# Causal scores of a chunked linear attention: one head per 32-row quarter of the TensorE array

## The chip, the core and the metric

The kernel runs on one core of a Trainium2 chip. The metric is the device time of one execution in microseconds. Engines are named as in the profile: PE is the TensorE matmul stream and PEld its weight loads, DVE is VectorE, ACT is ScalarE, POOL is GpSimd, SP is the engine that issues the DMAs.

## What is computed

One transformer layer over x of shape (2, 4096, 256) in float32: linear attention with 8 heads of 32 features in chunks of 64 tokens, then a mixture of 8 experts. The change touches only `scores`, which are masked causally inside a chunk.

```python
def step(state, inp):                      # b: 2 batches, h: 8 heads, c, e: 64 tokens of a chunk, d: 32 features
    qq, kk, vv = inp
    inter  = jnp.einsum('bhcd,bhde->bhce', qq, state)
    scores = jnp.einsum('bhcd,bhed->bhce', qq, kk) * mask     # mask = tril(ones(64, 64))
    intra  = jnp.einsum('bhce,bhed->bhcd', scores, vv)
    state  = state + jnp.einsum('bhcd,bhce->bhde', kk, vv)
    return (state, inter + intra)
...
x = x + _layernorm(attention(_layernorm(x)))
gate, up = x_n @ Wg[e], x_n @ Wu[e];  out = sum_e weights[e] * ((silu(gate) * up) @ Wd[e])
x = x + _layernorm(out)
```

## The kernel before

The 4096 rows of each batch are cut into 16 blocks of 256 rows, so a block holds 512 tokens, in four tiles of 128. A tile is half a block (`p` = 0 or 1) of one batch (`b`), and holds two chunks (`i` = 0 or 1). A software pipeline runs two blocks at once: while PE does the eight experts of block i-1, it does the attention of block i in between. The order is written out by hand: the list `STEPS` has 28 slots of attention steps, and `rest` (called in each engine's loop over the blocks) puts slots 4e-4+2m and 4e-3+2m between the products of expert e, half m. On PE one such turn is `up(e, m)` (gate and up products, 12 matmuls of 512 moving columns), a slot, `down(e-1, m)` (12 matmuls of 256 columns), a slot. Attention operands are plain fp32; the products with weights are float32r in three terms (high by high, low by high, high by low). A plain fp32 matmul that is no transpose leaves two weight loads and two matmuls in the trace: 64 matmuls are 128 records.

The steps around the change, in the order of the slots, and where they stand in the turns:
- `("kt", 0), ("kt", 1)` after `up(2, 1)`: PE transposes the keys (L530); ACT copies them out of PSUM to `kz` twice (L743), scaled by `odd_even[:, 0]` and by `odd_even[:, 1]`. These scales are 1 and 0 on alternating groups of 32 partitions, so copy `j` keeps only one head of each pair of heads and has zeros for the other.
- `("su", 0), ("su", 1)` after `up(3, 0)`: PE makes each chunk's key-value product (L573), DVE adds it to the running `state` (L951) and counts up `state_ready`.
- `("s", 0), ("s", 1)` after `up(3, 1)`: the scores. A matmul (L544) has 64 rows (two heads, one of them zeroed in `kz`), 64 stationary columns (the keys of a chunk) and 64 moving columns (its queries). Half `r` of the array's rows takes one pair of heads and writes bank `r` of two PSUM banks; chunk `i` takes half `i` of the output partitions. So four 64x64 tiles of the array are used in turn. A step has 2 (b) x 4 (n) x 2 (i) x 2 (r) = 32 matmuls. DVE multiplies each step's 128x1024 scores by the mask (L936) and counts up `prob_ready`.
- `("o", 0), ("o", 1)` after `up(4, 0)`: outputs, from the state and the queries (`with_state`, L446, 66 moving columns) and from the masked scores and the values (L461, 33 moving columns), also in 64x64 tiles.

PSUM: the attention has four banks, `att_ps`. Successive steps take banks 0 and 1, then 2 and 3, by turns (`att_half`), and each waits until the step before the last has been read out (`READ_OUT`). Block 0 has orders of its own (`FIRST_PE`, `FIRST_ACT`, `FIRST_DVE`), in which the two score steps stand apart from each other; `is_first(a)` tells it from the 15 other blocks.

Of the kernel before, what the change touches and what calls it, by code (L numbers as in the profile page):

```python
# [8 lines left out]

# [2 lines left out]

# [4 lines left out]
B, S, HID = 2, 4096, 256  # L19
H, D = 8, 32  # L20
E, INNER = 8, 256
P = 128
KT = HID // P
HG = H * D // P
# [92 lines left out]
def build_program(nc, x, wq_t, wkv_t, wo_t, norm_w, wg, wu, wd, wr, temperature, out):  # L117
# [4 lines left out]
    with ctx:  # L122
# [152 lines left out]
        def reach(eng, count, block, k):  # L275

            s, per_block, first = count
            base, offset = block
            value = offset * per_block + k + first
            if isinstance(base, int):  # L280
                if base * per_block + value > first:
                    eng.wait_ge(s, base * per_block + value)  # L282
            else:
                eng.wait_ge(s, base * per_block + value)
# [24 lines left out]
        def att_half(step, a):  # L309
# [3 lines left out]
                return att_ps[:, 2 * n, :]  # L313
            return att_ps[:, 2 * n:2 * n + 2, 0:256 if is_first(a) and step[0] == "q" else columns]

        def is_first(a):
            return psum_order(a) is FIRST_PSUM_STEPS


        def prob_of(p, a):  # L320
            return probs[1 - p if is_first(a) else p]


        def is_last(f):
# [107 lines left out]
        def _(pe):  # L432
# [19 lines left out]
            def o_own(p, dst, a):  # L452
                for b in range(B):
                    for x in range(2):
                        with_state(p, dst, b, x, x)
                for b in range(B):
                    for j in range(HPG):
                        for g in range(HG):
                            for i in range(2):
                                chunk, c = slice(C * i, C * i + C), b * HPG * VA + j * VA  # L460
                                last = nc.tensor.matmul(dst[C * g:C * g + C, i, c:c + VA],  # L461
                                                        prob_of(p, a)[chunk, j // 2, b, 2 * g + j % 2, :],
                                                        v_sb[chunk, 2 * p + b, g * HPG + j, :], start=False, stop=False)
                return last

# [14 lines left out]
            def att_step(step, a):  # L480
# [1 line left out]
                    return  # L482
                kind, dst, number = step[0], att_half(step, a), number_of(step, a)

                if number >= 2:
                    count, k = READ_OUT[psum_order(a)[number - 2]]
                    reach(pe, count, a, k)
                else:
                    count, k = READ_OUT[PSUM_STEPS[N_PSUM - 2 + (number + N_PSUM) % 2]]
                    reach(pe, count, (a[0], a[1] - 1), k)  # L490
# [41 lines left out]
                elif kind == "s":  # L532
                    p = step[1]
                    reach(pe, q_ready, a, p + 1 if is_first(a) else HG)
                    reach(pe, kz_ready, a, p + 1)
                    pe.sem_inc(quarters_begun, 1)
                    for b in range(B):
                        for n in range(2 * HG):
                            g, j = divmod(n, 2)
                            for i in range(2):  # L540
# [5 lines left out]
                                                            start=True, stop=True)  # L546
                elif kind == "o":
                    p = step[1]
                    reach(pe, prob_ready, a, p + 1)
                    reach(pe, v_ready, a, p + 1)  # L550
                    reach(pe, state_ready, a, p + 1)
                    pe.sem_inc(quarters_begun, 1)
# [154 lines left out]
        def _(act):  # L707
# [18 lines left out]
            def att_step(step, a):  # L726
# [9 lines left out]
                elif kind == "kv":  # L736
# [2 lines left out]
                    copy(v_sb[:, ts, :, 0:D], src[:, :, HID:2 * HID].rearrange("p b (h d) -> p b h d", h=H))\  # L739
                        .then_inc(v_ready[0], 1)  # L740
                elif kind == "kt":
                    for j in range(2):
                        last = nc.scalar.activation(kz[:, step[1], :, j, :], src, ACT.Copy, scale=odd_even[:, j:j + 1])  # L743
                    last.then_inc(kz_ready[0], 1)
# [150 lines left out]
        def _(dve):  # L895
# [5 lines left out]
            def low(dst, src, high_part):  # L901
                return nc.vector.tensor_tensor(dst, src, high_part.bitcast(f32), ALU.subtract)  # L902
# [22 lines left out]
            def att_step(step, a):  # L925
                kind = step[0]
                if kind == "xt":
# [2 lines left out]
                    lo, hi = (xt[:, :, half] if is_first(a) else halves(xt[:, k, :]) for xt in (xt_lo, xt_hi))  # L930
                    reach(dve, xt_hi_ready, a, k + 1)
                    low(lo, att_half(step, a), hi).then_inc(xt_ready[0], 1)
                elif kind == "s":
                    reach(dve, att_done, a, number_of(step, a) + 1)
                    each = [P, 2, 4 * HG, C]
# [416 lines left out]
```

## Time and profile before

| | |
|---|---|
| median of 3 runs | 1487.56 us (1487.32 to 1488.09) |
| the profiled execution | 1487.54 us |
| its span, first to last instruction | 1485.8 us |
| PE busy | 1462.7 us, 98% of the span, 14438 matmul records |
| DVE, ACT, POOL busy | 1003.5, 632.5, 427.4 us |
| granted TensorE clock, mean | 0.997 |

The profiled execution and the median are 0.02 us apart, so a sum made on the one holds for the other. The busy time of an engine is a union: records that overlap count once. A PE row of the timeline gives the start of its first record, the time to the modelled end of its last one, and the number of records; the distance between the starts of two neighbouring rows is how long the first of them held up the stream.

### The profile page before, as it was taken

What the parts mean: (1) busy time and instruction counts of PE and PEld (TensorE: products, weight loads), DVE (VectorE), ACT (ScalarE), POOL (GpSimd) and SP (SyncE); (2) the same over time, 40 slices, a digit from 0 to 9 for tenths busy, and PEclk for the clock granted to TensorE, in tenths of its full rate; (3) what the DMA queues carried; (4) which work ended last, traced back from release to release, by engine and by line L of the source; (5) the groups of instructions that cost most, each with busy time, mean ns of one, the idle gap of its engine ahead of it and who ended that gap; (6) DMA issues with size and microseconds to landing.
All of it is one profiled execution on the core that took longest, in us unless ns stands there. A gap on an engine that the chain in (4) does not pass through costs nothing. (4 is left out here: it accounts for less than half of the span.)

```text
span 1485.8 us, 37233 instructions
## 1 busy us (share of the span) xinstructions
PE 1462.7 (98%) x14438; PEld 1276.4 (86%) x14438; DVE 1003.5 (68%) x2397; ACT 632.5 (43%) x1157; POOL 427.4 (29%) x621
## 2 busy tenths in 40 slices
PE   7899999999999999999999999999999999999997
PEld 7788888888888888888888888888888888888886
DVE  6748567576676767667586675766667676675765
ACT  5434534444344443534435343443434445344332
POOL 1402414123241322414133141232413124141230
PEclk9999999999999999999999999999999999999999
DMA  5100000000000000000000000000000000000000
GB/s 172 58 2 15 14 0 14 14 14 14 0 28 0 14 14 14 14 0 14 14 14 14 0 14 14 14 14 0 28 0 14 14 14 14 0 15 16 2 8 22
DMA packets 25345, 24.59 MB, mean 17 GB/s; under 512 B 2016, under 2 KB 25056, under 8 KB 25312
## 3 DMA queue, kind: packets, MB, share of 16 engines
q1 hardware_dynamic: 25312, 24.13, 5.1%
q8 instruction: 23, 0.38, 0.1%
q14 instruction: 10, 0.08, 0.0%
HBM read 15.74 MB, written 8.39 MB: 16 GB/s over the span
## 5 line engine op out<-in xcount | busy, mean ns | idle before, releaser
L1013 DVE TENSOR_TENSOR late<-late,up_ps 128x512 f32<-128x512 f32 x256 | 174.9, 683 | 153.7 <-PE up_ps L440 149.3
L790 ACT ACTIVATE late<-gate_ps 128x512 f32<-128x512 f32 x256 | 152.6, 596 | 278.8 <-PE gate_ps L440 277.7
L440 PE MATMUL down_ps<-w_hi,h_hi 128*128 128x256 f32 x976 | 264.6, 293 | 0.0
L709 ACT ACTIVATE h_hi<-late 128x512 fp32r<-128x512 f32 x256 | 161.4, 630 | 222.0 <-DVE late L1013 221.9
L440 PE MATMUL down_ps<-w_hi,h_lo 128*128 128x256 f32 x976 | 253.9, 282 | 0.0
L1247 POOL TENSOR_TENSOR rms_in<-rms_in,minus_half 128x16 f32<-128x16 f32 x32 | 93.4, 2918 | 493.7 <-DVE rms_in L961 493.7
L902 DVE TENSOR_TENSOR h_lo<-late,h_hi 128x512 fp32r<-128x512 f32 x256 | 175.7, 686 | 65.4 <-ACT h_hi L709 65.4
L1035 DVE SCALAR_TENSOR_TENSOR late<-down_ps,route,late 128x256 f32<-128x256 f32 x364 | 158.6, 477 | 90.3 <-PE down_ps L440 87.8
L440 PE MATMUL gate_ps<-ft_hi,w_hi 128*128 128x512 f32 x512 | 204.0, 398 | 1.4 <-ACT ft_hi L709 0.8
L440 PE MATMUL gate_ps<-ft_hi,w_lo 128*128 128x512 f32 x512 | 203.0, 396 | 0.0
L440 PE MATMUL up_ps<-ft_hi,w_hi 128*128 128x512 f32 x512 | 199.7, 390 | 0.0
L440 PE MATMUL up_ps<-ft_hi,w_lo 128*128 128x512 f32 x512 | 199.5, 390 | 0.0
L440 PE MATMUL down_ps<-w_lo,h_hi 128*128 128x256 f32 x976 | 196.5, 283 | 0.0
L440 PEld LDWEIGHTS down_ps<-w_hi,h_hi 128*128 128x128 f32 x976 | 184.8, 189 | 10.5 <-issue 3.0
L440 PEld LDWEIGHTS down_ps<-w_hi,h_lo 128*128 128x128 f32 x976 | 185.8, 190 | 4.4
L440 PE MATMUL gate_ps<-ft_lo,w_hi 128*128 128x512 f32 x512 | 159.0, 392 | 0.0
L440 PE MATMUL up_ps<-ft_lo,w_hi 128*128 128x512 f32 x512 | 157.7, 389 | 0.0
L440 PEld LDWEIGHTS down_ps<-w_lo,h_hi 128*128 128x128 f32 x976 | 151.5, 191 | 0.0
L440 PEld LDWEIGHTS gate_ps<-ft_lo,w_hi 128*128 128x128 f32 x512 | 96.5, 188 | 21.9
L440 PEld LDWEIGHTS up_ps<-ft_hi,w_hi 128*128 128x128 f32 x512 | 96.4, 188 | 21.1
L440 PEld LDWEIGHTS up_ps<-ft_hi,w_lo 128*128 128x128 f32 x512 | 96.4, 188 | 20.1
L440 PEld LDWEIGHTS up_ps<-ft_lo,w_hi 128*128 128x128 f32 x512 | 96.2, 188 | 20.0
(172 smaller groups left out, 2420.6 us busy)
## 6 DMA issues: line engine op xcount, KB each, us to landing
xs<-in_x SPq DMA_DIRECT2D x32, 256.0 KB, 2.9
out_rows<-late SPq DMA_DIRECT2D x32, 256.0 KB, 2.2
late<-in_wg SPq DMA_DIRECT2D x7, 256.0 KB, 3.3
late<-in_wu SPq DMA_DIRECT2D x7, 256.0 KB, 4.3
late<-in_wd SPq DMA_DIRECT2D x6, 256.0 KB, 4.4
late<-in_wkv_t SPq DMA_DIRECT2D x1, 512.0 KB, 4.1
x<-in_wd SPq DMA_DIRECT2D x2, 256.0 KB, 5.2
late<-in_wq_t SPq DMA_DIRECT2D x1, 256.0 KB, 4.6
```

The costliest lines, as they stand in the source:

```text
L440: last = nc.tensor.matmul(dst, lhs, rhs, start=n == 0, stop=n == len(terms + low_terms) - 1)
L709: return nc.scalar.activation(dst, src, ACT.Copy)
L790: nc.scalar.activation(h_f[:, m, :], gate_ps[:, :], ACT.Silu).then_inc(silu_ready[0], 1)
L902: return nc.vector.tensor_tensor(dst, src, high_part.bitcast(f32), ALU.subtract)
L1013: nc.vector.tensor_tensor(h_f[:, m, :], h_f[:, m, :], up_ps[m][:, :], ALU.mult).then_inc(h_ready[0], 1)
L1035: last = nc.vector.scalar_tensor_tensor(dst[:, t, :], src, route[:, t, e:e + 1], acc[:, t, :], ALU.mult, ALU.add)
L1247: nc.gpsimd.tensor_tensor(rms_f[:, p, :, :], rms_in[:, p, :, :], minus_half[:, :, :], ALU.pow)\
```

## The change

For all blocks but the first, a score matmul takes one head alone, on 32 rows: head `j` of a group of four lies on the 32 partitions of row quarter `j`, and its scores go to PSUM bank `j`. Chunk `i` still takes output half `i`, so eight 32x64 tiles of the array are used in turn: four quarters for chunk 0, four for chunk 1. Both halves `p` lie side by side in the four banks, columns 0 to 255 and 256 to 511, so the two steps together fill `att_ps`. The number of matmuls stays: 2 (b) x 2 (g) x 2 (i) x 4 (j) = 32 a step. Since no head has to be zeroed, ACT copies the transposed keys to `kz` once, unscaled. The waits follow the banks: both score steps wait until all four banks are free (`state_ready` 2), DVE masks neither half before both steps are done on PE, and the output steps wait until both halves are masked. The masked scores get another layout in SBUF, `prob_block`. The first block stays as it was.

```diff
--- before.py
+++ after.py
@@ -9,6 +9,7 @@
 
 
 
+import itertools
 import math
 from contextlib import ExitStack
 
@@ -313,12 +314,23 @@
                 return att_ps[:, 2 * n, :]
             return att_ps[:, 2 * n:2 * n + 2, 0:256 if is_first(a) and step[0] == "q" else columns]
 
+
+        def score_banks(p):
+            return att_ps[:, :, 256 * p:256 * p + 256]
+
         def is_first(a):
             return psum_order(a) is FIRST_PSUM_STEPS
 
 
         def prob_of(p, a):
             return probs[1 - p if is_first(a) else p]
+
+
+        def prob_block(p, a, chunk, b, g, j):
+            if is_first(a):
+                return prob_of(p, a)[chunk, j // 2, b, 2 * g + j % 2, :]
+            return prob_of(p, a).rearrange("p r b n c -> p (r b n c)").rearrange("p (j b g c) -> p j b g c", j=HPG, b=B,
+                                                                                 g=HG)[chunk, j, b, g, :]
 
 
         def is_last(f):
@@ -459,7 +471,7 @@
                             for i in range(2):
                                 chunk, c = slice(C * i, C * i + C), b * HPG * VA + j * VA
                                 last = nc.tensor.matmul(dst[C * g:C * g + C, i, c:c + VA],
-                                                        prob_of(p, a)[chunk, j // 2, b, 2 * g + j % 2, :],
+                                                        prob_block(p, a, chunk, b, g, j),
                                                         v_sb[chunk, 2 * p + b, g * HPG + j, :], start=False, stop=False)
                 return last
 
@@ -482,7 +494,10 @@
                     return
                 kind, dst, number = step[0], att_half(step, a), number_of(step, a)
 
-                if number >= 2:
+                if kind in ("s", "o") and not is_first(a):
+
+                    pass
+                elif number >= 2:
                     count, k = READ_OUT[psum_order(a)[number - 2]]
                     reach(pe, count, a, k)
                 else:
@@ -533,8 +548,16 @@
                     p = step[1]
                     reach(pe, q_ready, a, p + 1 if is_first(a) else HG)
                     reach(pe, kz_ready, a, p + 1)
+                    if not is_first(a):
+
+                        reach(pe, state_ready, a, 2)
                     pe.sem_inc(quarters_begun, 1)
-                    for b in range(B):
+                    for b, g, i, j in itertools.product(range(0 if is_first(a) else B), range(HG), range(2), range(HPG)):
+                        head, c = slice(D * j, D * j + D), b * P + C * i
+                        tok, out_c = 2 * p * P + c, (b * HG + g) * C
+                        last = nc.tensor.matmul(score_banks(p)[C * i:C * i + C, j, out_c:out_c + C], kz[head, p, g, 0, c:c + C],
+                                                q_t[head, g, tok:tok + C], start=True, stop=True)
+                    for b in range(B if is_first(a) else 0):
                         for n in range(2 * HG):
                             g, j = divmod(n, 2)
                             for i in range(2):
@@ -546,7 +569,7 @@
                                                             start=True, stop=True)
                 elif kind == "o":
                     p = step[1]
-                    reach(pe, prob_ready, a, p + 1)
+                    reach(pe, prob_ready, a, p + 1 if is_first(a) else 2)
                     reach(pe, v_ready, a, p + 1)
                     reach(pe, state_ready, a, p + 1)
                     pe.sem_inc(quarters_begun, 1)
@@ -739,6 +762,9 @@
                     copy(v_sb[:, ts, :, 0:D], src[:, :, HID:2 * HID].rearrange("p b (h d) -> p b h d", h=H))\
                         .then_inc(v_ready[0], 1)
                 elif kind == "kt":
+                    if not is_first(a):
+                        copy(kz[:, step[1], :, 0, :], src).then_inc(kz_ready[0], 1)
+                        return
                     for j in range(2):
                         last = nc.scalar.activation(kz[:, step[1], :, j, :], src, ACT.Copy, scale=odd_even[:, j:j + 1])
                     last.then_inc(kz_ready[0], 1)
@@ -930,6 +956,15 @@
                     lo, hi = (xt[:, :, half] if is_first(a) else halves(xt[:, k, :]) for xt in (xt_lo, xt_hi))
                     reach(dve, xt_hi_ready, a, k + 1)
                     low(lo, att_half(step, a), hi).then_inc(xt_ready[0], 1)
+                elif kind == "s" and not is_first(a):
+
+                    reach(dve, att_done, a, number_of(("s", 1), a) + 1)
+                    each = [P, HPG, B * HG, C]
+                    nc.vector.tensor_tensor(prob_of(step[1], a).rearrange("p r b n c -> p (r b n c)")
+                                            .rearrange("p (j n c) -> p j n c", j=HPG, c=C),
+                                            score_banks(step[1]).rearrange("p j (n c) -> p j n c", c=C),
+                                            causal[:, :, :].unsqueeze(1).broadcast_to(each), ALU.mult)\
+                        .then_inc(prob_ready[0], 1)
                 elif kind == "s":
                     reach(dve, att_done, a, number_of(step, a) + 1)
                     each = [P, 2, 4 * HG, C]
```

The rows that follow are the built programs' order, each engine for itself, with the semaphores that an instruction waits for. On PE, around the two score steps, `att_ps<-q_t,kz`, between `up(3, 1)` and `down(2, 1)`. Before:

```order
L440 MATMUL up_ps<-ft_lo,w_hi 128x512 [waits ft_ready]
L440 MATMUL up_ps<-ft_lo,w_hi 128x512
L544 MATMUL att_ps<-q_t,kz 64x64 [waits kz_ready,state_ready,q_ready]
L544 MATMUL att_ps<-q_t,kz 64x64 x31
L544 MATMUL att_ps<-q_t,kz 64x64 [waits kz_ready,state_ready,q_ready]
L544 MATMUL att_ps<-q_t,kz 64x64 x31
L284 REGISTER_ALU [waits h_lo_ready]
L440 MATMUL down_ps<-w_hi,h_hi 128x256 [waits down_read]
```

And with the change:

```order
L452 MATMUL up_ps<-ft_lo,w_hi 128x512 [waits ft_ready]
L452 MATMUL up_ps<-ft_lo,w_hi 128x512
L558 MATMUL att_ps<-q_t,kz 64x64 [waits state_ready,q_ready,kz_ready]
L558 MATMUL att_ps<-q_t,kz 64x64 x31
L558 MATMUL att_ps<-q_t,kz 64x64 [waits state_ready,q_ready,kz_ready]
L558 MATMUL att_ps<-q_t,kz 64x64 x31
L285 REGISTER_ALU [waits h_lo_ready]
L452 MATMUL down_ps<-w_hi,h_hi 128x256 [waits down_read]
```

The 64 matmuls keep their place and number, and the names waited for are the same. What differs is the count: `("s", 0)` now waits for the second of the two state steps.

On ACT, at the copies of the transposed keys, `kz<-att_ps`, between the SiLU of expert 2's second half and the copy `h_hi` behind it. Before:

```order
L790 ACTIVATE late<-gate_ps 128x512 [waits h_lo_ready]
L284 REGISTER_ALU
L743 ACTIVATE kz<-att_ps,odd_even 128x2x256 [waits att_done]
L743 ACTIVATE kz<-att_ps,odd_even 128x2x256
L284 REGISTER_ALU
L743 ACTIVATE kz<-att_ps,odd_even 128x2x256 [waits att_done]
L743 ACTIVATE kz<-att_ps,odd_even 128x2x256
L709 ACTIVATE h_hi<-late 128x512 [waits down_done,h_ready]
```

With the change:

```order
L816 ACTIVATE late<-gate_ps 128x512 [waits h_lo_ready]
L285 REGISTER_ALU
L732 ACTIVATE kz<-att_ps 128x2x256 [waits att_done]
L285 REGISTER_ALU
L732 ACTIVATE kz<-att_ps 128x2x256 [waits att_done]
L732 ACTIVATE h_hi<-late 128x512 [waits down_done,h_ready]
```

Two of the four copies are gone; `h_hi` moves up by two instructions.

On DVE, at the masks, between expert 3's product `late<-late,up_ps` and the low half `h_lo`. Before:

```order
L1013 TENSOR_TENSOR late<-late,up_ps 128x512 [waits up_done,silu_ready]
L284 REGISTER_ALU
L936 TENSOR_TENSOR rows<-att_ps,causal 128x1024 [waits att_done]
L284 REGISTER_ALU
L936 TENSOR_TENSOR shared<-att_ps,causal 128x1024 [waits att_done]
L1035 SCALAR_TENSOR_TENSOR late<-down_ps,route,late 128x256 [waits down_done]
L1035 SCALAR_TENSOR_TENSOR late<-down_ps,route,late 128x256
L902 TENSOR_TENSOR h_lo<-late,h_hi 128x512 [waits h_hi_ready]
```

With the change:

```order
L1048 TENSOR_TENSOR late<-late,up_ps 128x512 [waits up_done,silu_ready]
L285 REGISTER_ALU
L963 TENSOR_TENSOR rows<-att_ps,causal 128x1024 [waits att_done]
L963 TENSOR_TENSOR shared<-att_ps,causal 128x1024 [waits att_done]
L1070 SCALAR_TENSOR_TENSOR late<-down_ps,route,late 128x256 [waits down_done]
L1070 SCALAR_TENSOR_TENSOR late<-down_ps,route,late 128x256
L928 TENSOR_TENSOR h_lo<-late,h_hi 128x512 [waits h_hi_ready]
```

The masks keep their place and their size, 128x1024. The register instruction between them, which made the count that the second mask waits for, is gone: both wait for the same count.

## Rows read from the trace of the kernel before

**Rows 1.** The page, its span, its engines and the granted clock in 40 slices.

```profile
span 1485.8 us, 37233 instructions
...
PE 1462.7 (98%) x14438; PEld 1276.4 (86%) x14438; DVE 1003.5 (68%) x2397; ACT 632.5 (43%) x1157; POOL 427.4 (29%) x621
...
PEclk9999999999999999999999999999999999999999
```

**Rows 2.** Busy time of each engine in one block's stretch, start of scores to start.

```profile
core 0: us, PE busy (x) PEld busy (x) DVE busy (x) ACT busy (x) POOL busy (x), PEclk, DMA share, GB/s
640.14:730.05 89.91, 89.91 (x895) 78.43 (x894) 61.37 (x147) 38.59 (x71) 26.67 (x38) 1.00 0.04 12
```

**Rows 3.** Records of the tile kz: count, duration in ns, first and last start.

```profile
L544 PEld LDWEIGHTS att_ps<-q_t,kz x2048: 129/135/135, 24.1 to 1361.7; 64*64 64x64 f32 x187
L544 PE MATMUL att_ps<-q_t,kz x2048: 218/218/267, 24.1 to 1361.8; 64*64 64x64 f32 x187
L743 ACT ACTIVATE kz<-att_ps,odd_even x64: 679/690/717, 22.6 to 1351.6; 128x512 f32<-128x512 f32 x64
```

**Rows 4.** Timeline of PE in one later block: start, us, what, records.

```profile
725.00 1.16 PE L573 MATMUL att_ps<-v_sb,k_sb 64*64 64x66 f32 x64
...
729.91 0.61 PE L440 MATMUL up_ps<-ft_lo,w_hi 128*128 128x512 f32 x2
730.46 2.12 PE L544 MATMUL att_ps<-q_t,kz 64*64 64x64 f32 x128
732.51 0.38 PE L440 MATMUL down_ps<-w_hi,h_hi 128*128 128x256 f32 x1
...
736.87 0.46 PE L446 MATMUL att_ps<-state,q_t 64*64 64x66 f32 x16
737.16 1.08 PE L461 MATMUL att_ps<-v_sb,rows 64*64 64x33 f32 x64
738.06 0.44 PE L446 MATMUL att_ps<-state,q_t 64*64 64x66 f32 x16
738.32 1.09 PE L461 MATMUL att_ps<-v_sb,shared 64*64 64x33 f32 x64
739.23 0.82 PE L446 MATMUL att_ps<-state,q_t 64*64 64x66 f32 x32
739.98 0.39 PE L440 MATMUL down_ps<-w_hi,h_hi 128*128 128x256 f32 x1
```

**Rows 5.** Timeline of PE, first block (score step, state step) and warming matmuls.

```profile
24.13 1.16 PE L544 MATMUL att_ps<-q_t,kz 64*64 64x64 f32 x64 [0.69 <-ACT kz L743]
...
26.85 0.70 PE L573 MATMUL att_ps<-v_sb,k_sb 64*64 64x66 f32 x32
...
47.65 4.52 PE L478 MATMUL gate_ps<-ident 128*128 128x128 f32 x39
```

**Rows 6.** Timeline of PE, router products of the same block, 128x32 tiles.

```profile
778.61 0.40 PE L601 MATMUL att_ps<-ft_lo,wr_pad 128*32 128x128 f32 x8
778.83 0.40 PE L601 MATMUL att_ps<-ft_hi,wr_pad 128*32 128x128 f32 x8
779.04 0.40 PE L601 MATMUL att_ps<-ft_lo,wr_pad 128*32 128x128 f32 x8
```

**Rows 7.** Weight loads of kz alone in two short stretches at the scores' start.

```profile
core 0: us, PEld busy (x), PEclk, DMA share, GB/s
730.46:730.48 0.03, 0.02 (x4) 1.00 0.00 0
730.48:730.51 0.03, 0.03 (x4) 1.00 0.00 0
```

**Rows 8.** Timeline of DVE from the state adds to the product behind the masks.

```profile
723.46 0.69 DVE L902 TENSOR_TENSOR h_lo<-late,h_hi 128x512 fp32r<-128x512 f32 x1 [0.22 <-ACT h_hi L709]
...
726.54 2.03 DVE L951 SCALAR_TENSOR_TENSOR state<-att_ps,odd_even,state 128x132 f32<-128x132 f32 x6
...
731.69 1.22 DVE L936 TENSOR_TENSOR rows<-att_ps,causal 128x1024 f32<-128x1024 f32 x1 [0.36 <-PE att_ps L544]
732.83 1.22 DVE L936 TENSOR_TENSOR shared<-att_ps,causal 128x1024 f32<-128x1024 f32 x1
734.24 0.88 DVE L1035 SCALAR_TENSOR_TENSOR late<-down_ps,route,late 128x256 f32<-128x256 f32 x2 [0.19 <-PE down_ps L440]
735.03 0.68 DVE L902 TENSOR_TENSOR h_lo<-late,h_hi 128x512 fp32r<-128x512 f32 x1
737.05 0.69 DVE L1013 TENSOR_TENSOR late<-late,up_ps 128x512 f32<-128x512 f32 x1 [1.34 <-PE up_ps L440]
```

**Rows 9.** Timeline of ACT at the copies of the transposed keys.

```profile
720.49 2.42 ACT L743 ACTIVATE kz<-att_ps,odd_even 128x512 f32<-128x512 f32 x4 [1.12 <-PE att_ps L530]
```

## The prediction, made blind

> **What bounds the kernel now.** Read first the page's engines [rows 1]: PE is busy for 1462.7 of 1485.8 us, and the clock reads 9 in all 40 slices, so the clock is not the subject. Then take one block by itself [rows 2]: from one start of the scores to the next are 89.91 us, and PE is busy in all of them, DVE in 61.4, ACT in 38.6. Fifteen of the sixteen blocks go like that. So PE's stream is the bound without a gap, and a microsecond taken out of it is a microsecond of the kernel, as long as no wait opens; a microsecond taken off ACT or DVE is worth nothing by itself.
>
> Next, how long the scores hold the stream [rows 4]: they start at 730.46, and `down` starts behind them at 732.51, so 2.05 us for 128 records; over the whole kernel these groups are 2048 records, 15 blocks of 128 and the first block's twice 64 [rows 3]. Fifteen times that is 31 us, about 2% of the kernel, and all that the change can take from is in it.
>
> **What sets the pace of the scores.** This decides the sum, so I take it from several rows.
>
> One score step alone, 64 records, has a row of 1.16 us [rows 5]; two steps, 128 records, have 2.12 [rows 4]. So 64 more records cost 0.96 us, 15.0 ns each, and 0.20 us is paid once. State products with 66 moving columns: 32 records 0.70 us [rows 5], 64 records 1.16 [rows 4], 14.4 ns each. Output products with 33 moving columns: 737.16 to 738.06 for 64 records [rows 4], 14.1 ns each. Half as many moving columns, and the same pace: so the columns that stream are not what binds.
>
> Now the whole array: 39 records of 128 stationary and 128 moving columns in 4.52 us [rows 5]. Less one duration (0.27) that is 4.25 / 38 = 112 ns each. A 64x64 tile has half the stationary columns, so on its own it should take about 56 ns; four tiles at once give 14.0. That is what the 64x64 rows show. In the router products the tiles are 32 columns wide and 128 columns move: 0.43 us for 16 records [rows 6], 27 ns each, again 112 / 4 = 28. So I read: each tile takes about 56 to 60 ns per record (here its weight load), and as many tiles work at once as there are tiles in turn, four in every row so far. The weight loads look like that too [rows 7]: four start within the first 25 ns of the scores, and none more in the next 30.
>
> **The change, part by part.**
>
> *The score matmuls.* Their number stays at 64 a block, 128 records, and so do 64 stationary and 64 moving columns; a record still costs its tile 56 to 60 ns. But there are now eight 32x64 tiles in turn. If all eight work at once, a record costs 14.0 / 2 to 15.0 / 2, I take 14.5 / 2 = 7.25 ns. Per block 128 x 7.25 = 0.93 us less. No row shows eight tiles at once, or 32-row quarters, so this price is bounded from both sides. Below: four loads start within 25 ns, some 6 to 8 ns from start to start [rows 7]; at 6.7 ns a record the gain would be 128 x 7.8 = 1.0 us. Above: if only two of the tiles in a column half worked at once and the other column half waited, 29 ns, a loss of 128 x 14.5 = 1.86 us. I take 7.25, because the price of one tile and the count of tiles have explained three shapes of tile (128x128, 128x32, 64x64), and the spacing of starts leaves room for eight in 56 ns. The amounts read at once do not grow either: two column halves times 128 partitions, before and after.
>
> Here the Trainium skill speaks against the change. Its page "TensorE: Matmul & The Clock Gate" (section "Wait — 56ns, not 53.3ns?") says that the distance between the starts of two matmuls never drops below about 25 ns, however small they are. By that rule 128 records would take 3.2 us, and no tiling could help. The trace does not agree: 14.1 to 15.0 ns in three groups of rows. The same page's section "Measured speedup vs the span model" has 4 row tiles at 3.07 times one, and 16 tiles at 10.6 times; no row here shows more than four.
>
> *Entering and leaving.* The 0.20 us paid once (filling, and the change to smaller tiles and back) I leave as it is: the tiles were small before.
>
> *The copies of the transposed keys.* Four copies in 2.42 us become two [rows 9], 1.2 us less on ACT a block, 18 us in all. Worth nothing: they end at 722.9, and the scores start at 730.46. What is next in that queue is `h_hi`, about a microsecond earlier; DVE waits 0.22 us for it [rows 8], and PE for neither.
>
> *The first score step waits for both state steps.* DVE ends its state adds at 728.57 [rows 8], PE comes to the scores at 730.46 [rows 4], with 1.9 us between. Nothing ahead of that point moves. Cost nothing; were the adds 1.9 us later, PE and all expert products behind it would stand.
>
> *Both masks wait for both steps.* DVE begins the first mask at 731.69 and ends the second at 734.05. The scores would end at 730.46 + 0.20 + 0.96 = 731.6, where they now end at 732.6: so the first mask starts where it does now although it waits for twice the work. Queued behind the masks are `add_down`, then the low half `h_lo`. `add_down` now waits 0.19 us for PE [rows 8]; `down` will be done earlier, so both start some 0.2 us sooner. A mask reads 256 columns of four banks in place of 512 of two; same 1024 elements, and I keep 1.22 us, with a tenth more or less as its bounds, which changes nothing.
>
> *The output steps wait for both masks.* PE comes to them at 736.87 now, at 735.94 then; the masks end at 734.05. The slack goes from 2.8 to 1.9 us. Were a mask 1 us longer, PE would wait here.
>
> *Other chains.* Only work that begins before the scores and is wanted after them loses 0.93 us of slack; the rest moves along with PE. The low half of expert 3 ends at about 735.5 and is wanted by `down(3, 0)` behind the outputs, at 739.98 less 0.93 [rows 4]. In a steady block PE shows no idle at all.
>
> *The first block* keeps its code.
>
> **Sum.** 15 blocks x 0.93 = 13.9 us from the profiled execution's 1487.54: 1473.6 us. The median of the runs is 1487.56, so the same number holds for it.
>
> **The rivals.**
>
> *Eight tiles, but a floor under them.* The starts within 25 ns come after a stretch in which instructions could queue up; over 256 instructions in a row PE may not be handed a load and a matmul every 7 ns. For it: the lowest pace held over a whole row is 14.1 ns. Against it: the pace did follow the tile's own time in every shape, with starts in a quick bunch and then a pause. A floor halfway, 10.9 ns, saves 128 x 3.6 = 0.46 us a block, 6.9 in all: 1480.6. Between 8 and 13 ns it gives 1475 to 1484.6.
>
> *The change doesn't do what it says: four at a time remain.* The number in flight may be a property of the engine, not of the tiles; four is all that any row shows. A record stays at 14.5 ns, the masks start 1 us later (their end at 735.0 against outputs at 736.87 hides it): 1487.5. The skill's 25 ns rule would end here too, since a floor that four tiles already reach leaves nothing to gain.
>
> *Slower: two at a time.* The order now puts four row quarters of one column half behind each other, then four of the other half. If quarters of one column half can share it only by twos, and PE does not look past them to the other half, a record costs 29 ns and a block 1.86 us more: 1487.5 + 27.8 = 1515.4. It decides from 14.5 ns a record on. Against it: `with_state` puts two tiles of one row half in a row, L461 two of one column half, and both hold the same pace: L446's 32 records hold the stream for 0.75 us with the change of shape in it [rows 4].
>
> **How the numbers follow.** Forecast 0.62, floor 0.18, four at a time 0.12, two at a time 0.08. The predicted time is the forecast's, 1473.6. Its own bounds are 6.7 ns (1472.5) and 8 ns (1475). The range goes from 1472 through the floor's cases to 1484.5 and holds 0.80; it leaves out no change and slower. A measurement of this kernel tells 0.2%, 3 us, from no change; so faster 0.80, same 0.12, slower 0.08.
>
> **What would show it.** In the changed profile: the row of the 128 score records at 1.1 to 1.2 us in place of 2.12, and `down` 1.1 us behind its start; a block at 89.0 us, with PE busy throughout; PE busy 14 us less in all; ACT 18 us less. A row of 1.6 us shows the floor, 2.1 four at a time, 4 two at a time. The masks should start 1.2 us after the scores' start as now; if PE idles ahead of L446's rows or ahead of the scores, one of the two added waits binds, and then my slacks of 1.9 us were wrong. The prediction fails most likely by the one price that no row shows, that of a record with eight tiles in turn.

## The result, and the profile after

The changed kernel takes 1482.63 us (median of 7 runs, 1481.39 to 1485.68), the kernel before 1487.95 (7 runs, 1487.32 to 1489.1). The ratio is 0.9968, 95% interval 0.9956 to 0.9979: faster by 5.3 us, which the interval holds clear of no change. The forecast was 13.9 us. The time lies inside the stated range of 1472 to 1484.5 us, but only because the range was drawn wide enough for the floor rival. The profiled execution took 1481.39 us, 6.15 less than the one before.

The page and one block's stretch of the changed kernel, to be held against [rows 1] and [rows 2]:

```profile
span 1479.7 us, 37189 instructions
...
PE 1456.3 (98%) x14438; PEld 1269.9 (86%) x14438; DVE 1000.7 (68%) x2397; ACT 612.6 (41%) x1127; POOL 431.6 (29%) x621
...
PEclk9999999999999999999999999999999999999999
```

```profile
core 0: us, PE busy (x) PEld busy (x) DVE busy (x) ACT busy (x) POOL busy (x), PEclk, DMA share, GB/s
637.37:726.89 89.52, 89.52 (x895) 78.05 (x893) 61.16 (x147) 37.28 (x69) 26.99 (x38) 1.00 0.04 12
```

A block, from one start of the scores to the next, went from 89.91 to 89.52 us, and PE is still busy in all of it. Fifteen times 0.40 is 6.0 us: the whole of the gain lies inside the blocks, and no new wait took part of it. It was not given back; it was smaller to begin with. PE's timeline around the scores shows where (start, us, what, records; [rows 4] before):

```profile
727.20 1.70 PE L558 MATMUL att_ps<-q_t,kz 32*64 32x64 f32 x128
728.84 0.39 PE L452 MATMUL down_ps<-w_hi,h_hi 128*128 128x256 f32 x1
...
733.21 0.46 PE L458 MATMUL att_ps<-state,q_t 64*64 64x66 f32 x16
```

The score row is 1.70 us, where 2.12 stood and 1.16 was forecast. DVE and ACT around it ([rows 8], [rows 9] before):

```profile
723.28 2.03 DVE L986 SCALAR_TENSOR_TENSOR state<-att_ps,odd_even,state 128x132 f32<-128x132 f32 x6 [0.15 <-DVEq L925]
...
728.94 1.23 DVE L963 TENSOR_TENSOR rows<-att_ps,causal 128x1024 f32<-128x1024 f32 x1 [0.87 <-PE att_ps L558]
730.08 1.22 DVE L963 TENSOR_TENSOR shared<-att_ps,causal 128x1024 f32<-128x1024 f32 x1
731.21 0.87 DVE L1070 SCALAR_TENSOR_TENSOR late<-down_ps,route,late 128x256 f32<-128x256 f32 x2
```

```profile
717.23 1.09 ACT L732 ACTIVATE kz<-att_ps 128x512 f32<-128x512 f32 x2 [1.12 <-PE att_ps L545]
```

How the pace runs inside the scores can be read by asking the timeline of the weight loads (PEld) for stretches that begin just ahead of the first load and end ever later: the count at the end of the row is how many loads have started by then. Here the stretches end 0.25, 0.50 and 0.75 us behind the first load. Before:

```profile
730.46 0.38 PEld L544 LDWEIGHTS att_ps<-q_t,kz 64*64 64x64 f32 x20 [0.35 <-issue]
...
730.46 0.62 PEld L544 LDWEIGHTS att_ps<-q_t,kz 64*64 64x64 f32 x36 [0.35 <-issue]
...
730.46 0.85 PEld L544 LDWEIGHTS att_ps<-q_t,kz 64*64 64x64 f32 x52 [0.35 <-issue]
```

With the change:

```profile
727.20 0.36 PEld L558 LDWEIGHTS att_ps<-q_t,kz 32*64 32x64 f32 x33 [0.35 <-issue]
...
727.20 0.62 PEld L558 LDWEIGHTS att_ps<-q_t,kz 32*64 32x64 f32 x49 [0.35 <-issue]
...
727.20 0.78 PEld L558 LDWEIGHTS att_ps<-q_t,kz 32*64 32x64 f32 x64 [0.35 <-issue]
```

Before, 20, 36, 52: an even 16 loads in each further quarter of a microsecond. With the change 33, 49, 64: the first quarter holds 33 loads, as eight tiles at once would have it, and then the pace is 15 to 16 per quarter, no better than before. Single starts in the trace say the same. The first 33 matmul records of a step start within 0.29 us; behind them the loads pause for about 0.13 us, then come stretches at 8.4 ns a record and stretches at 17; and the 65th record, the first of the second step, comes 106 ns behind the 64th.

### The profile page after: what moved, and what is told of

Same layout as the page of the kernel before. It is cut to its first block and busy times, and to the rows that moved or that the text cites. A ratio compares the mean times of both kernels' runs of the same rounds, so it can differ in the third digit from the quotient of the medians.

```text
span 1479.7 us, 37189 instructions
## 1 busy us (share of the span) xinstructions
PE 1456.3 (98%) x14438; PEld 1269.9 (86%) x14438; DVE 1000.7 (68%) x2397; ACT 612.6 (41%) x1127; POOL 431.6 (29%) x621
```

## The experiments

Theories. **F**, feeding: eight tiles do work at once, but PE is handed loads and matmuls slower than these tiles take them; about 32 records stand ready when the scores begin, the rest comes as it is handed on. **A**: batch 1's addresses are slow. **D**: row quarters of one column half share it by twos. **N**: neighbouring matmuls in one column half hinder each other. **Q**: the loss belongs to row quarters or to four banks at once. **T**: tiles are slowed by leftover work of earlier tiles. **J**: the waits between the two score steps cost. And the added waits and the copies, which were priced at nothing.

Each time below is a single execution, except that of `a_join`; the changed kernel's own seven executions differ by 4.3 us. The rows and the length of a block tell more: in the steady blocks of a trace they repeat to a few hundredths of a microsecond.

**Order of the same matmuls.** In `a_gb` the loops run g, b, i, j in place of b, g, i, j, in `a_ij` g, b, j, i (the ranges are shortened here to what they are in the 15 later blocks).

```diff
-for b, g, i, j in itertools.product(range(B), range(HG), range(2), range(HPG)):
+for g, b, i, j in itertools.product(range(HG), range(B), range(2), range(HPG)):      # a_gb
+for g, b, j, i in itertools.product(range(HG), range(B), range(HPG), range(2)):      # a_ij
```

> The changed kernel with the loop over the head groups g outside and that over the batches b inside: the same 64 score matmuls a block in another order. Theory F (a stock of 32 records, then handed on slowly): nothing changes, 32 records fast and 32 slow, row 1.70 us, time within 1 us of the changed kernel's 1481.4. Rival A (batch 1's addresses are slow): runs of 16 fast and 16 slow records alternate; sum and time the same, but the pattern inside the step is another.

> The changed kernel with the chunks i inside and the heads j outside of them, so that neighbouring matmuls take the two column halves of one row quarter, then the next quarter: same 64 matmuls a block, same eight tiles in turn. Theory F (feeding): no difference, row 1.70 us, period 89.51 us, time within 1 us of the changed kernel's. Rival N (neighbours in one column half hinder each other, as in the slower case of the prediction): the row gets shorter, by the 0.1 us of each stall or more.

Measured: 1482.26 and 1481.72 us. Timelines of PE, of `a_gb` and then of `a_ij`:

```profile
728.03 1.71 PE L558 MATMUL att_ps<-q_t,kz 32*64 32x64 f32 x128
```

```profile
727.28 1.71 PE L558 MATMUL att_ps<-q_t,kz 32*64 32x64 f32 x128
```

Not only the rows are the same. The starts of every eighth record lie within 3 ns of the changed kernel's (0, 106, 165, 223, 291, 458, 537, 604 ns in the first step), with the slow part behind the 32nd record each time, whichever batch and column half it belongs to. A and N fall.

**Four quarters of one column half.** `a_onehalf` leaves out chunk i = 1.

> The changed kernel without the scores of the second chunk of each 128 tokens (i = 1 is left out in the 15 later blocks, so half of the score work is missing): four 32x64 tiles in turn, all in one column half, 64 records a block. Forecast of the tile price: four row quarters of one column half work at once, one tile takes 58 ns a record, so 14.6 ns a record, score row about 1.15 us, 0.55 us less a block than the changed kernel, 1473 us. Rival D (quarters of one column half share it by twos): 29 ns a record, row about 2.0 us, 1486 us. Theory F has no say at 14.6 ns, since that is slower than it hands on.

Measured: 1475.13 us. PE's row, and the load counts at 0.25 and 0.50 us:

```profile
725.37 1.16 PE L558 MATMUL att_ps<-q_t,kz 32*64 32x64 f32 x64
```

```profile
725.36 0.38 PEld L558 LDWEIGHTS att_ps<-q_t,kz 32*64 32x64 f32 x20 [0.35 <-issue]
...
725.36 0.61 PEld L558 LDWEIGHTS att_ps<-q_t,kz 32*64 32x64 f32 x36 [0.35 <-issue]
```

1.16 us for 64 records, to the hundredth what 64 records of four 64x64 tiles take [rows 5], and the same counts of 20 and 36. So a tile of a row quarter costs what a 64x64 tile does, 58 ns a record, and four quarters in one column half do work at once. D falls, and the tile price of the prediction stands.

**Eight tiles without quarters.** `b_eight` is the kernel before with 64x32 tiles, eight in turn (the edit in short).

```diff
-for n in range(2 * HG):              # dst[C*i : C*i+64, r, ...],  kz[half, ..., c : c+64]
+for n in range(HG):
     ...
+    for h in range(2):               # dst[C*i+32*h : ... +32, r, ...],  kz[half, ..., c+32*h : ... +32]
```

> The kernel before with eight tiles of 64 rows and 32 columns in turn in place of four of 64x64: a score matmul of the 15 later blocks takes 32 keys and 64 queries of a head pair, and half of the scores is left out so that it stays at 128 records a block. No row quarters, two banks. It tells whether the eight tiles or the row quarters make the slow part. Theory F (feeding): eight tiles in turn take a record every 7.3 ns, the stock of 32 is gone, then stalls and 8.4 to 12 ns as in the changed kernel: row 1.70 us, block period about 89.5 us, time about 1481.5. Rival Q (the stall behind the 32nd record, 128 ns longer than in the run with small matmuls in four tiles, belongs to row quarters): no such stall, row 1.4 to 1.5 us, period 89.25 us, time about 1478.

Measured: 1480.32 us. PE's row, and the load counts at 0.25, 0.50 and 0.75 us:

```profile
727.12 1.62 PE L557 MATMUL att_ps<-q_t,kz 64*32 64x64 f32 x128
```

```profile
727.12 0.30 PEld L557 LDWEIGHTS att_ps<-q_t,kz 64*32 64x32 f32 x33 [0.35 <-issue]
...
727.12 0.60 PEld L557 LDWEIGHTS att_ps<-q_t,kz 64*32 64x32 f32 x54 [0.35 <-issue]
...
727.12 0.85 PEld L557 LDWEIGHTS att_ps<-q_t,kz 64*32 64x32 f32 x65 [0.35 <-issue]
```

33, then 54, then 65: the fast start and the fall of pace behind it come without a row quarter and with two banks instead of four. The stall that Q gave to the row quarters is there too: behind the 33rd load two gaps of 77 and 56 ns, where the changed kernel has 70 and 59. The row of 1.62 us is 0.08 short of the changed kernel's and 0.12 above what Q named, so Q falls as the main cause; 0.08 us a block may still belong to the shape.

**Short work for each tile.** `b_small` (four tiles of the kernel before) and `a_small` (eight row-quarter tiles) take 32 keys and 32 queries in each matmul.

> The kernel before (head pairs on 64 rows, four tiles in turn) with only the first 32 keys and 32 queries of each chunk in the score matmuls of the 15 later blocks, so three quarters of the scores are missing: 128 records a block as ever, but 32 stationary and 32 moving columns each, so a tile is free again after about half the time. It makes short work for a tile without any row quarter. Theory F (feeding): the same loss of pace as in the changed kernel appears without row quarters: 32 records fast, then 8 to 9 ns each with stalls, row about 1.7 us in place of 2.12, time about 1481.5. Rival Q (the loss belongs to row quarters or to four banks at once): the pace follows the tile, about 7 to 8 ns a record throughout, row about 1.2 us, time about 1474.

> The changed kernel with only the first 32 keys and 32 queries of each chunk in the score matmuls of the 15 later blocks (three quarters of the scores missing): row quarters, eight tiles in turn, each free again after half the time. Theory F: the tiles no longer matter, the first 32 records come as close as starts can, 6 to 7 ns, and behind them the pace is what PE is handed: the row stays between 1.6 and 1.75 us, time about 1481.5. If instead the slow part belongs to the time of the tiles, it halves: row about 1.2 us, time about 1474.5.

Measured: 1478.05 and 1478.15 us. PE's row of each, `b_small` first, with the load counts of `a_small` at 0.13, 0.25, 0.50 and 0.75 us behind:

```profile
726.16 1.47 PE L545 MATMUL att_ps<-q_t,kz 64*32 64x32 f32 x128
```

```profile
725.77 1.47 PE L558 MATMUL att_ps<-q_t,kz 32*32 32x32 f32 x128
```

```profile
725.77 0.23 PEld L558 LDWEIGHTS att_ps<-q_t,kz 32*32 32x32 f32 x30 [0.35 <-issue]
...
725.77 0.34 PEld L558 LDWEIGHTS att_ps<-q_t,kz 32*32 32x32 f32 x34 [0.35 <-issue]
...
725.77 0.59 PEld L558 LDWEIGHTS att_ps<-q_t,kz 32*32 32x32 f32 x60 [0.35 <-issue]
...
725.77 0.84 PEld L558 LDWEIGHTS att_ps<-q_t,kz 32*32 32x32 f32 x68 [0.35 <-issue]
```

Both expectations missed the size, and the pair says more than each. Both kernels need 1.47 us, though one has twice the tiles of the other, each half as long busy as in the changed kernel. In `a_small` the first 30 loads start within 0.13 us of the first one, 4 ns apart, and then PE has to wait: 34 after 0.25 us. So there is a floor that no tile sets, (1.47 - 0.19) / 128 = 10 ns a record over two steps (0.19 is the duration of one record here), and a stock of about 32 records ahead of it. In both kernels 0.16 to 0.17 us of it lie between the two steps, and the 64 records of one step start within 0.56 us, 8.9 ns apart.

The place of the stall says the same. The 33rd load of the first step starts 134 ns after the first in `a_small`, 195 in `b_eight`, 227 in the changed kernel and 245 in `b_small`, each as its tiles allow; the 34th starts after 244, 272, 297 and 277 ns. The first 33 differ by 111 ns, the next one by 53: it comes when it is handed on, nearly whatever the tiles do.

The changed kernel's 1.70 us lies 0.23 above that floor. Each of its steps takes about 0.13 us longer to start its 64 records, and its gap between the steps is 0.05 to 0.06 shorter. Its tiles' own 7.3 ns and the supply's pauses may add up in part instead of hiding each other; no run isolates that.

**Twice the matmuls.** `a_twice` and `b_twice` issue each step's score matmuls twice over, on the changed kernel and on the one before.

> The changed kernel with the score matmuls of each step issued twice over (same operands, same outputs) in the 15 later blocks: 256 records a block in place of 128, nothing left out. The question is where the changed kernel loses pace inside a step. Its trace shows a step's first 32 records at 7.3 ns each and the other 32 at over 12. Theory F (feeding): a stock of instructions stands ready when a step begins and is used up after 32 records; from then on PE is handed a record every 8 to 9 ns. Then the second pass has no fast part, 64 more records cost some 0.54 us a step, the score row goes from 1.70 to about 2.8 us, the time from 1481.4 to about 1498. Rival A (addresses): what is slow is the second half of a step, batch 1, by where its operands or outputs lie. Then fast and slow alternate a second time: 0.70 us more a step, the row about 3.1 us, the time about 1502.

> The kernel before with the score matmuls of each step issued twice over in the 15 later blocks: 256 records a block, four 64x64 tiles in turn, nothing left out. Beside the changed kernel doubled, which took 4.5 to 5.0 us for its 256 records with a pause of some 2 us ahead of about the 160th. Theory F with a supply that a pace of 14.6 ns a record doesn't exhaust: no pause, 128 more records cost 1.87 us, the row goes from 2.12 to about 3.99 us, the time from 1487 to about 1515. If the supply of instructions falls behind even that pace over a long stretch, pauses of 1 to 2 us show here too, and the row is 5 us or more, the time about 1530.

Measured: 1541.43 and 1536.95 us, 60 and 49 us above the kernels that they double. For `a_twice` 17 to 21 were expected; for `b_twice` 28, or 43 if pauses of 1 to 2 us showed, and they do. PE's timeline in one block of `a_twice`, and what the whole kernel's waits say:

```profile
195.57 1.97 PE L558 MATMUL att_ps<-q_t,kz 32*64 32x64 f32 x159
199.05 1.26 PE L558 MATMUL att_ps<-q_t,kz 32*64 32x64 f32 x97 [1.52 <-issue]
```

```profile
PE att_ps L558 <- issue: 24.5, 15, 2.1
```

The same of `b_twice`:

```profile
194.42 2.58 PE L544 MATMUL att_ps<-q_t,kz 64*64 64x64 f32 x159
197.91 1.67 PE L544 MATMUL att_ps<-q_t,kz 64*64 64x64 f32 x97 [0.91 <-issue]
199.50 0.39 PE L440 MATMUL down_ps<-w_hi,h_hi 128*128 128x256 f32 x1
```

```profile
PE att_ps L544 <- issue: 15.8, 14, 1.6
```

In 14 of the 15 later blocks of both, PE stops behind the 159th record, idle with nothing that the profile shows to wait for ("issue"), and goes on 3.37 to 4.06 us after the scores began in `a_twice` and 3.49 to 4.15 us in `b_twice`, although one came to that place in 1.97 us and the other in 2.58. Again the tiles do not set it. The trace shows what does. The profile counts the packets of a DMA queue of instructions; first the changed kernel's line, then that of `a_twice`, and `b_twice` has the same one:

```profile
q8 instruction: 23, 0.38, 0.1%
```

```profile
q8 instruction: 143, 2.34, 0.6%
```

The only code that grew is PE's, by 256 loads and matmuls a block, and this queue alone grew with it, so it carries PE's instructions; the other instruction queue stays at 10 packets. A steady block of the changed kernel has 1786 loads and matmuls in its trace, and no packet of instructions moves in that kernel between 151 and 1330 us: its blocks run from what was loaded before. With 2042 loads and matmuls, 9 packets of 16384 bytes move in a steady block. One of them falls into the scores. In the block of `a_twice` shown above it moves from 196.67 to 197.80 us, and PE (first column behind the length) goes on 1.25 us after it landed. The last columns are the DMAs' share and GB/s; 14 GB/s over 1.21 us is that packet:

```profile
core 0: us, PE busy (x) PEld busy (x) DVE busy (x) ACT busy (x) POOL busy (x), PEclk, DMA share, GB/s
195.57:196.60 1.03, 1.03 (x99) 1.03 (x101) 0.69 (x1) 0.13 (x1) 0.00 (x0) 1.00 0.00 0
196.60:197.81 1.21, 0.94 (x87) 0.80 (x71) 0.00 (x0) 0.50 (x1) 0.00 (x0) 1.00 0.06 14
197.81:199.05 1.24, 0.00 (x0) 0.00 (x0) 0.00 (x0) 0.00 (x0) 0.00 (x0) 1.00 0.00 0
```

Over all 29 pauses of the two runs PE goes on 1.24 to 1.61 us after such a packet has landed. In the last block the packets fall elsewhere, and so does the pause: in `a_twice` it stands behind the 130th record, and `b_twice` has none there and a row of 3.98 us, which is the 3.99 that F named. No run moved a packet on purpose, but these two blocks did it by themselves. So this second, longer pause is the loading of PE's instructions, and it is not part of the changed kernel's time, whose steady blocks load none.

For the short pauses the same run refutes A once more: the second pass has no fast part. Its pace (the first step's records 33 to 128 take 11.4 ns each) is what F named as 8 to 9, so F had the sign and not the size. And the short pauses are not this loading, since they stand in blocks without a packet.

**The gap between the two steps.** `a_join` drops the waits and the marker increment ahead of the second step. The edit, shortened to what holds in the 15 later blocks:

```diff
-reach(pe, q_ready, a, HG);  reach(pe, kz_ready, a, p + 1);  reach(pe, state_ready, a, 2);  pe.sem_inc(quarters_begun, 1)
+if p == 0:
+    reach(pe, q_ready, a, HG);  reach(pe, kz_ready, a, 2);  reach(pe, state_ready, a, 2);  pe.sem_inc(quarters_begun, 1)
```

> The changed kernel in which the second score step has no waits and no marker increment of its own in the 15 later blocks: the first one waits for both halves of kz at once, and PE goes from the 64th to the 65th record without an instruction in between that is no load or matmul. In the changed kernel's trace the 65th record comes 106 ns behind the 64th, where neighbours stand 7 to 17 ns apart. Theory J (the two waiting instructions between the steps cost the gap): the gap goes, the second step has no fresh fast part, some 0.1 us less a block, 1.5 us in all, about 1480. Theory F alone (PE is handed instructions at a given pace on average, and the pause is where it catches up): the gap closes but the records behind it come slower by as much, and the time stays within 1 us of the changed kernel.

Measured over five rounds: 1480.91 us (1480.15 to 1482.0), ratio to the kernel before 0.9956, interval 0.9942 to 0.9969. PE's timeline:

```profile
726.86 1.59 PE L559 MATMUL att_ps<-q_t,kz 32*64 32x64 f32 x128
728.39 0.39 PE L452 MATMUL down_ps<-w_hi,h_hi 128*128 128x256 f32 x1
```

The row is 0.11 us shorter and a block 89.40 us long in place of 89.52, so 1.7 us in all: J holds, and the part of F that said the supply would take it back does not. The 65th record now starts 17 ns behind the 64th and not 106, and the second step has no fast part: its 33rd load starts 0.36 us after its first, where the changed kernel has 0.25. That is a puzzle for F. In the changed kernel a stock of 32 records stands ready again behind a gap of only 0.13 us in the loads, in which a supply of one record every 8.4 ns would hand on 15. How the stock fills, no run shows.

`a_join` has the lowest time of the kernels that compute the whole of it. Its time and the changed kernel's (1480.15 to 1482.0 against 1481.39 to 1485.68) were not taken side by side and overlap a little; the length of a block does not.

**A step each in two slots.** `a_split` moves the second score step behind `down(2, 1)`.

> The changed kernel with the first score step in the slot where both were, and the second one slot later, behind the 12 matmuls of down(2, 1); DVE makes both masks where it made the first. Same records, nothing left out. Theory F (a stock of 32 records is ready when a stretch of scores begins, then records are handed on slower): each part runs like the changed kernel's first step, a row of about 0.89 us for 64 records with the stall behind the 32nd. The gap of 106 ns between the steps goes, but entering and leaving the small tiles is paid twice, about 0.23 us: a block gets about 0.1 us longer, time about 1483. Rival T (what slows is the tiles themselves, such as leftover work of earlier tiles): the second part would look like the changed kernel's second step, with its other pattern.

Measured: 1489.95 us. PE's timeline:

```profile
732.10 0.91 PE L558 MATMUL att_ps<-q_t,kz 32*64 32x64 f32 x64
732.94 0.39 PE L452 MATMUL down_ps<-w_hi,h_hi 128*128 128x256 f32 x1
...
734.57 0.91 PE L558 MATMUL att_ps<-q_t,kz 32*64 32x64 f32 x64
```

Both parts are alike, 0.91 us, each with its fast 32 and its pause, which is F's and not T's picture. But the price of going in and out again was set too low: a block is 89.77 us long, 0.25 more and not 0.1. With the gap of 0.106 that is saved, the second entry and exit cost about 0.35 us, and not 0.23. The 0.25 us make 3.8 of the 8.5 us that the profiled spans are apart. Another 4.0 are idle in "issue" ahead of L473 and L567 in three places, which the changed kernel's trace doesn't have. They too are loading: each ends 1.3 to 1.5 us after a packet of instructions landed, near 31, 112 and 1370 us, outside the steady stretch between 151 and 1330 us.

**What was priced at nothing.** `b_waits` puts only the waits of the change into the kernel before, `a_kz2` gives ACT its two extra copies back.

> The kernel before with only the waits of the change in the 15 later blocks: both score steps wait for both state steps, both masks for both score steps, the output steps for both masks. The matmuls, banks and copies stay. Expected: no idle of PE in a steady block, the block's period stays at 89.91 us, time 1487.5, within 0.5 us. If one of the added waits binds, the period grows, up to 0.9 us a block (both masks later by one step), and the missing gain of the change would be part of it.

> The changed kernel with two copies of the transposed keys again, the second one to the unused half of kz, so ACT does 1.2 us more a block as before the change. Expected: nothing moves, block period 89.51 us as in the changed kernel, time within 1 us of it, since ACT is done with the copies 5 us before the scores. If ACT's work did count, the period would grow by up to 1.2 us.

Measured: 1487.81 us, beside 1487.8 for the kernel before measured with it, and 1481.99 us. One block of `b_waits`, then one of `a_kz2`, each from one start of the scores to the next:

```profile
640.27:730.19 89.92, 89.92 (x898) 78.45 (x897) 61.28 (x147) 38.59 (x71) 26.67 (x38) 1.00 0.04 12
```

```profile
638.08:727.60 89.52, 89.52 (x895) 78.05 (x894) 61.19 (x147) 38.22 (x71) 26.68 (x38) 1.00 0.04 12
```

89.92 and 89.52 us: the length of the kernel before and of the changed one, with PE busy throughout. `a_kz2` gives ACT back 0.94 us a block (38.22 against 37.28) of the 1.3 that the change took off. Both prices were right.

## Why the prediction missed

**PE is the bound, and a microsecond of it is one of the kernel: right.** The row fell by 0.42 us, the block by 0.40, the profiled time by 6.15, all the same gain.

**The price of a tile and the number of tiles at once: right, for as long as there is something to do.** The 33rd load of the scores starts 0.23 us after the first, 7.1 ns a record, where 7.25 was forecast for all. `a_onehalf` shows the tile's 58 ns, `b_eight` the eight tiles without quarters.

**The price of a record over 128 of them: this step failed.** I took 7.25 ns and the row shows (1.70 - 0.20) / 128 = 11.7. The term of the sum was 15 x 0.93 = 13.9 us and is 15 x 0.40 = 6.0. Its lower bound came from [rows 7], four starts in 25 ns, and four starts say how close starts can come, not how long that can be kept up. The chip keeps it up for 32 records behind a wait. Behind them the kernel before shows no such limit, since 14.5 ns a record lies above it: the rows from which I took the price were all slower than the supply that now decides. The rival "a floor under them" named the place and the reason (a stock filled during the stretch before, then 256 instructions in a row); its halfway value of 10.9 ns gave 1480.6, and the medians say 1482.6. It had 0.18 and should have had the larger share. Starts 7 ns apart come in bunches of four to six in the trace before, and the closest 33 starts anywhere in it stand 13.7 ns apart on the average. That the time fell inside the range is that rival's doing and no merit of the forecast.

**The masks start where they did: wrong by the same 0.5 us.** They start 1.74 us after the scores, not 1.23. (The prediction's end of the scores at 731.6 also took 0.96 us for the 128 records where its own price gives 0.93; nothing hangs on it.) The slack held all the same: the second mask ends at 731.30 and the output steps start at 733.21, 1.9 us, as forecast, and the state adds end at 725.31 for scores at 727.20, again 1.9.

**ACT 18 us less: 19.9.** The two copies take 1.09 us where four took 2.42. Not only their number fell: a copy without the scale from SBUF takes 592 to 598 ns and one with it 679 to 717, and neighbours overlap by about 0.1 us.

**The Trainium skill's floor of 25 ns between starts** ("TensorE: Matmul & The Clock Gate", "Wait — 56ns, not 53.3ns?") does not hold here in this form: 33 loads in 0.23 us, and 10 ns a record over 128. The rival that some floor limits what more tiles give was right in kind, and nearer to the result than the forecast; its place is 10 to 12 ns, and the change still gained.

**Left open.** What hands on the records after the first 32 of a step is open. The loading of instructions from memory it is not, since no packet of them moves in a steady block; loading explains only the long pauses, in the doubled kernels and in `a_split`. How a stock of 32 is there again behind a gap of 0.13 us is open too, and so is why the changed kernel's row stands 0.23 us above the floor of the runs with short work.

## What to carry to other kernels

When a stream of small matmuls is bound by its tiles, more tiles in turn gave the full factor here for the first 32 records behind a wait only; price a run of 128 at 10 to 12 ns a record on the average, or ask how few instructions do the work. A price that is worked out from rows slower than the next limit doesn't contain that limit: look for the longest stretch in which the trace held the pace that the sum needs, and give the rival its chance by that. Instructions that only wait or count, put between two runs of small matmuls, cost about 0.1 us each time once the stream is short of supply (`a_join`); in the kernel before, the 65th record comes 39 ns behind the 64th, as between any two bunches, and they cost nothing. Before more instructions go into a loop, look at the packets of the instruction queue: a loop that moves none may begin to load part of itself in every round.

## What the hardware showed that was not expected

- For the first 32 records behind a wait, small matmuls start as close together as their tiles allow, down to 4 ns (30 loads in 0.13 us with eight 32x32 tiles). Behind them they come 8.4 ns apart in the better stretches, and 10 to 12 ns apart on the average of 128.
- With 1786 loads and matmuls in a block, no packet of instructions moves in the steady blocks; with 2042, nine of 16 KB move in each. One that falls into the scores stops PE for 0.9 to 2.1 us, until 1.2 to 1.6 us after it has landed: doubling 2 us of small matmuls cost 49 us over 15 blocks, not 28.
